# Causal attention: both halves of the turned probabilities copied by VectorE in the steps that do not end a tile

## What is computed

```python
att = jnp.einsum('bhqd,bhkd->bhqk', q, k) * hd ** (-0.5)
att = jnp.where(causal, att, -jnp.inf)
att = jax.nn.softmax(att, axis=-1)
y = jnp.einsum('bhqk,bhkd->bhqd', att, v).transpose(0, 2, 1, 3).reshape(Bb, T, C)
return y @ wo + bo
```

## Time and profile before

| | us |
|---|---|
| median of three runs | 1734.31 |
| lowest and highest run | 1730.68, 1734.47 |
| the profiled execution | 1724.97 |
| its span on the core | 1723.42 |
| TensorE matmul busy | 1594.9 |
| TensorE weight loads busy | 1322.6 |
| VectorE busy | 741.0 |
| ScalarE busy | 680.1 |
| GpSimd busy | 240.4 |
| mean granted TensorE clock over the span | 0.961 of full speed |

### The profile page before, as it was taken

One profiled execution on the slowest core, in us unless ns is written; L12 is line 12 of the kernel. 1 busy time (PEld: TensorE's weight loads), 2 busy tenths in 40 slices (PEclk: granted clock), 3 DMA queues, 4 the chain that ended last, 5 costly groups with the idle time before them and its releaser, 6 DMA issues.

```text
span 1723.4 us, 32899 instructions
## 1 busy us (share of the span) xinstructions
PE 1594.9 (93%) x12477; PEld 1322.6 (77%) x12477; DVE 741.0 (43%) x2621; ACT 680.1 (39%) x2160; POOL 240.4 (14%) x378
## 2 busy tenths in 40 slices
PE   7999989889999999999689988989999999999986
PEld 5787877689986777777488877878987777777765
DVE  2635445521025666755111137553114444344457
ACT  2614423322105757556133317543324443244432
POOL 2012200000001121211411123128000000000000
PEclk9999999989999999989699989889999999999998
DMA  9500011238601010400498920206850001000000
GB/s 324 195 1 2 1 40 37 85 108 304 139 1 52 11 44 2 176 2 2 157 321 300 318 97 23 99 31 217 300 175 1 1 1 37 1 2 1 2 1 22
DMA packets 103255, 156.41 MB, mean 91 GB/s; under 512 B 12231, under 2 KB 80959, under 8 KB 102535
## 3 DMA queue, kind: packets, MB, share of 16 engines
q1 hardware_dynamic: 97515, 143.53, 25.5%
q0 software_dynamic: 3552, 9.18, 1.6%
q10 hardware_dynamic: 2048, 1.84, 0.3%
HBM read 147.31 MB, written 11.67 MB: 92 GB/s over the span
## 4 chain that ended last, share of the span: by engine, by line
PE 66%; ACT 8%; DVE 5%; issue 3%; DMA 2%; POOL 1%; SPq 1%; DVEq 0%; ACTq 0%; POOLq 0%
PE psum L567 42%; PE psum L638 5%; ACT arena L839 5%; PE psum L622 4%; PE psum L662 4%; PE psum L916 3%; PE psum L523 3%; DMA moe_b<-in_moe_b 2%; POOL token_rows L1217 1%; PE psum L903 1%; PE psum L670 1%; DVE arena L756 1%; ACT arena L851 1%; PE psum L908 0%; SPq L985 0%
## 5 line engine op out<-in xcount | busy, mean ns | idle before, releaser
L839 ACT ACTIVATE arena<-arena,rowmin 112x375 f32<-112x375 f32 (+1 forms) x584 | 292.8, 508 | 179.3 <-DVE rowmin L756 179.1
L567 PE MATMUL psum<-arena,region 128*128 128x112 f32 (+2 forms) x1920 | 325.8, 328 | 6.5 <-DMA arena<-in_ctxT 2.5
L567 PEld LDWEIGHTS psum<-arena,region 128*128 128x128 f32 x1920 | 263.2, 197 | 69.8 <-issue 8.1
L567 PE MATMUL psum<-region,arena 128*125 128x128 f32 (+4 forms) x1632 | 234.4, 293 | 16.5 <-DVE arena L1986 4.8
L567 PEld LDWEIGHTS psum<-region,arena 128*125 128x125 f32 (+2 forms) x1632 | 197.2, 184 | 51.5 <-issue 19.3
L638 PEld LDWEIGHTS psum<-identity,arena 112*125 112x125 f32 (+1 forms) x1240 | 142.4, 177 | 63.7 <-ACT arena L851 17.2
L638 PE MATMUL psum<-identity,arena 112*125 112x112 f32 (+1 forms) x1240 | 169.2, 279 | 18.8 <-ACT arena L851 5.0
L567 PE MATMUL psum<-arena 128*128 128x128 f32 (+4 forms) x896 | 138.2, 312 | 0.8 <-DMA moe_b<-in_moe_b 0.8
L622 PE MATMUL psum<-arena 32*112 32x375 f32 (+3 forms) x912 | 133.5, 477 | 0.5 <-DVE arena L734 0.4
L567 PEld LDWEIGHTS psum<-arena 128*128 128x128 f32 (+2 forms) x896 | 124.0, 189 | 12.1 <-issue 1.6
L897 POOL COPY arena<-rinv 112x128 f32<-112x128 f32 x136 | 34.0, 293 | 595.2 <-DVE rinv L776 571.3
(11 more groups left out here) (298 smaller groups left out, 1871.3 us busy)
## 6 DMA issues: line engine op xcount, KB each, us to landing
stream<-in_moe_w SPq DMA_DIRECT2D x36, 1024.0 KB, 7.4
arena<-in_moe_w SPq DMA_DIRECT2D x36, 1024.0 KB, 7.3
arena<-in_ctxT SPq DMA_DIRECT2D x32, 375.0 KB, 4.0
stream<-in_e_wg SPq DMA_DIRECT2D x8, 512.0 KB, 4.4
stream<-in_e_wu SPq DMA_DIRECT2D x8, 512.0 KB, 5.5
stream<-in_e_wd SPq DMA_DIRECT2D x8, 512.0 KB, 6.6
region<-in_e_wg SPq DMA_DIRECT2D x8, 512.0 KB, 7.5
region<-in_e_wu SPq DMA_DIRECT2D x8, 512.0 KB, 8.2
```

The lines of the kernel that those rows point to most:

```text
L567: last = pe.matmul(dst, l, r, start=(i == 0), stop=(i == n - 1))
L839: last = act.activation(e, e, ACT.Exp, bias=rowmin[:, j, n:n + 1], scale=-1.0, accum_out=rowsum[:, j, h:h + 1])
```

## The change

In `attend_vector`, `keep_rest(r)` first copies the half of sequences 0 and 1 out of bank 4 and signals `probs_T`, and then does its own copy out of bank 5, if r is not the last step of its tile. In `attend_scalar`, `keep_probs(r)` does nothing for these steps. The last step of a tile is done as before: ScalarE copies bank 4 and VectorE bank 5.

```diff
--- before.py
+++ after.py
@@ -764,6 +764,9 @@
                 if r >= 2:
                     v.wait_ge(*p["probs_used"].at(it, r - 2))
                 if a.whole_pairs:
+                    if r % a.steps + 1 < a.steps:
+                        v.tensor_copy(a.turned(r)[0:T, 0:2, 0:2 * T], three(bank[4][0:T, 0:4 * T], 2))\
+                            .then_inc(p["probs_T"].sem, 1)
                     dst, src = a.turned(r)[0:T, 2:4, 0:2 * T], three(bank[5][0:T, 0:4 * T], 2)
                 else:
                     n = a.key_tiles - 1
@@ -841,6 +844,8 @@
                 last.then_inc(p["probs"].sem, 1)
 
             def keep_probs(r):
+                if a.whole_pairs and r % a.steps + 1 < a.steps:
+                    return
                 act.wait_ge(*p["probs_turned"].at(it, r))
                 if r >= 2:
                     act.wait_ge(*p["probs_used"].at(it, r - 2))
```

## The result

Six runs of each kernel were timed in turn: the changed kernel took 1721.13 us (median; 1719.80 to 1725.84), the kernel before 1732.74 (1730.68 to 1734.47). The ratio is 0.994, 95% interval 0.9927 to 0.9953: 0.6% faster, 10 to 12 us. The prediction had the direction and what the copies do, but less than a third of the size: 3.1 us, with 1725 as the lowest time. The profiled execution took 1721.13 us, its span 1719.6.

What follows compares the result with a forecast made beforehand. ScalarE was taken to pace the steps at 3.39 us, TensorE 0.44 behind. A -1.5, B and D -1.2 each and C +0.8 gave -3.1 us, from the median 1734.31 to 1731.2 us; range 1725 to 1737.

Steps and rivals of the forecast that it cites:

- C: Layer 1's attention over the first four sequences; first tile gains 0.82 us, second loses 1.59, together +0.8 us.
- A: Layer 0's attention over the first four sequences, with two normalisations on VectorE; forecast -1.5 us.
- B: Layer 0's attention over the second four sequences; first tile 0, second tile -1.23, together -1.2 us.
- D: Layer 1's attention over the second four sequences, with gates' arithmetic like B; forecast -1.2 us.
- B's gates: Gates' arithmetic on VectorE after step 1, 1.39 us, leaves no idle time; B's first tile gains 0.
- the case against: C's second tile: VectorE also adds tokens and paces it, so three more copies make it 1.59 us later.
- it hangs on where things fall, and I leave it out of the sum: Low clock in closings of A and C, costing 1.7 us in A; outside the sum, two stretches either way in range.
- The prediction's own sign of the clock: If the total moves over 5 us while the attentions move 3, the clock did it; closings' granted clock shows it.
- Of the rivals, the first: Clock comes back: three falls vanish (A, C and one more), gain 8.2 us, 1726.1 us; chance 0.2.
- The second: Clock falls further: C's wait grows, B's luck ends, two more slow stretches, +0.3 us, 1734.6 us; chance 0.15.
- The third: VectorE paces every tile through the pair of copies ahead of the masks: +12.7 us, 1747.0 us; chance 0.06.
- the fourth: Nothing arrives: weight transfers behind C and D set the experts' pace, 1734.3 us; chance 0.07.

Runs made afterwards that it cites:

- before_pad8: Kernel before plus eight padding products ahead of each attention's last transposes, no copy moved; ratio 0.9955, 1714.70 us against 1723.55.
- layer0_only: Kernel before with the copies moved in attentions A and B alone; ratio 0.9961 to the kernel before.
- layer1_only: Kernel before with the copies moved in attentions C and D alone; ratio 0.9994 to the kernel before.
- after_again: The changed kernel once more, unchanged; ratio 0.9957 to the kernel before, 1715.19 us.
- base_again: The kernel before once more, unchanged; ratio 1.0003 to the kernel before.
- look_before: A further profile of the unchanged kernel before, a single execution; 1733.64 us.
- change_only: The changed kernel again, unchanged, on another chip; ratio 0.994 to the kernel before (1731.34 us).
- pad_only: Same kernel as before_pad8 (eight padding products per attention, no copy moved), measured again; ratio 0.9944 to the kernel before (1731.34 us).

## Why the prediction was wrong

*The copies: right in their working, 1.4 us too small in sum.* These are starts read from the timelines, relative to the attention's first exponential. Without falls or the long C:

| | predicted | measured | from |
|---|---|---|---|
| A, first tile | -0.8 | -0.86 | second tile starts at 18.05, before 18.91 |
| A, second tile | -0.7 | -0.71 | to the last transposes 13.35, before 14.06 |
| B, first tile | 0 | -0.25 | 18.67, before 18.92 |
| B, second tile | -1.23 | -1.27 | 12.79, before 14.06 |
| C, first tile | -0.82 | -1.10 | 18.04, before 19.14 |
| C, second tile | +1.59 | +1.58 | 17.17, before_pad8 15.59 |
| D | -1.2 | -1.9 | last transposes at 31.47, before 33.33 |
| sum | -3.1 | -4.5 | |

The pair costs 2 x 0.53 us, which was the value taken; neither the dependence between the two copies nor slower reads of PSUM appeared. The Trainium skill, VectorE: DVE Perf Modes, section Specifications, puts ScalarE closer to PSUM and VectorE closer to SBUF; 0.53 against 0.41 us agrees in sign, but ScalarE was the one that paced, so the dearer engine was the right one.

A's second tile runs at 3.26 us a step as computed for VectorE with its normalisations (starts at 21.60, 24.86 and 28.12). B's gates come out as the working had them: the eight transposes were to start 9.55 us behind B's first exponential (779.87 less 770.32); they start at 9.58, 775.87 less 766.29. VectorE and TensorE's weight loads in B answer to the earlier trace rows:

```profile
773.26 0.29 DVE L2136 TENSOR_TENSOR arena<-expert_number,gate_small 112x32 f32<-112x32 f32 x2
...
774.65 0.62 DVE L768 COPY arena<-psum 112x448 f32<-112x448 f32 x1
775.18 0.61 DVE L774 COPY arena<-psum 112x448 f32<-112x448 f32 x1
```
```profile
775.87 0.76 PEld L638 LDWEIGHTS psum<-identity,arena 112*112 112x112 f32 x8 [0.61 <-DVE arena L768]
776.78 0.35 PEld L662 LDWEIGHTS psum<-arena 112*32 112x32 f32 x16
```

Of B's extra 0.25, 0.09 is there when these transposes are done (the outputs behind them start 10.49 us into B, before 10.58). The other 0.15 comes where the next transposes stand behind the key and query products: from one set of outputs to the next it was 3.41 us before (780.90 to 784.31, with a part of a wait for exponentials) and is 3.26 now (776.78 to 780.04). I had argued that nothing after the key and query products waits; something still did.

Of C's 1.10 in the first tile, 0.22 us aren't its copies': its second step starts 3.30 us after its first instead of 3.52. It does so in layer0_only too, where C has no copy moved, and doesn't in layer1_only, where it has; what C's own copies give there is 0.88. In the kernel before VectorE pauses 0.2 us between two of the masks (1044.64 to 1045.05, where two usually start 0.2 apart). Of D's 1.9, 0.36 us aren't its copies' either: in layer0_only, where D has none moved, D's second tile also starts 0.36 earlier (18.92, before 19.27). So some 0.6 of the 4.5 us came with the change but not from an attention's own copies, and why is open.

C's second tile is the case against, and it came true to 0.01 us. The exponentials of after_again start 4.45 us apart (1066.00 to 1070.45), before 3.92. Its weight loads answer to the earlier trace rows, the wait of 2.54 us is now 3.04. The profile puts it down to line 768, but TensorE waits for both copies, and the second, line 774, is the last to be ready: it starts at 1073.75, and the transposes 0.69 us later.

```profile
1068.88 0.62 DVE L768 COPY arena<-psum 112x448 f32<-112x448 f32 x1
1069.42 0.61 DVE L774 COPY arena<-psum 112x448 f32<-112x448 f32 x1
...
1073.23 0.60 DVE L768 COPY arena<-psum 112x448 f32<-112x448 f32 x1
1073.75 0.61 DVE L774 COPY arena<-psum 112x448 f32<-112x448 f32 x1
```
```profile
1071.04 0.35 PEld L662 LDWEIGHTS psum<-arena 112*32 112x32 f32 x16
1074.44 0.76 PEld L638 LDWEIGHTS psum<-identity,arena 112*112 112x112 f32 x8 [3.04 <-DVE arena L768]
```

*The step that failed: "it hangs on where things fall, and I leave it out of the sum".* The clock term was set to zero in the sum, as a matter of luck, with two stretches either way in the range. It is a term with a sign. Of the kernel before, three profiles have a fall in A's closing three times, in B's twice and in D's twice. Of the changed kernel, four profiles have none in A, B or D; C's stays. On one chip, base_again is 7.8 us longer in the four attentions than after_again (160.23 less 152.45), 4.5 by the copies and 3.3 by the falls of A and B. Against after_again, the first profile of before is 7.7 us longer in the four attentions (160.18 less 152.45): 4.5 of these are the copies; falls are the other 3.2 (A 1.7, D 1.6, C -0.1, which stays). B's fall, where it occurs, adds 1.6. The profiles with the long C differ by 9.1 us in the four attentions (look_before 170.34, change_only 161.20). Of these, 4.5 are again the copies, so the falls make 3.2 to 4.6 us, which the sum had at nothing. The medians differ by 7.1 us on the chip without the long C and by 11.6 and 10.9 on two where it occurs, so up to 2.5 us lie in stretches that the change doesn't touch. There executions of the same kernel differ by as much: the changed kernel has 38 to 44 us at 1.2 GHz before A, and A starts between 708.9 and 712.0, so I don't explain them. The prediction's own sign of the clock, a total that moves by more than 5 us while the attentions move by 3, came in kind: the total moved by 11.6, the copies by 4.5.

What TensorE did ahead of the closings goes with their clock. In the last step of A in the kernel before it waited 1.22 us for ScalarE's copy and then twice for exponentials, 2.14 us in all:

```profile
742.45 0.19 PEld L638 LDWEIGHTS psum<-identity,arena 112*112 112x112 f32 x2 [0.37 <-ACT arena L839]
743.19 0.19 PEld L638 LDWEIGHTS psum<-identity,arena 112*112 112x112 f32 x2 [0.55 <-ACT arena L839]
```

In the changed kernel the first wait is a little longer, but all of them together are 1.65 us:

```profile
740.24 0.57 PEld L638 LDWEIGHTS psum<-identity,arena 112*112 112x112 f32 x6 [1.36 <-DVE arena L768]
741.10 0.18 PEld L638 LDWEIGHTS psum<-identity,arena 112*112 112x112 f32 x2 [0.29 <-ACT arena L842]
```

So the change shortened two things: these last waits, and the 0.44 us that TensorE stood still in each step before them. Counted over all 18 profiles, by the sum of the waits in the last step:

| closings | waits in the last step, us | with a fall |
|---|---|---|
| C, not padded | 2.54 to 3.07 | 11 of 11 |
| A, B, D, copies not moved | 2.14 | 8 of 12 (A 4 of 4, B and D 2 of 4 each) |
| A, B, D, copies moved | 1.60 to 1.65 | 0 of 21 |
| all four, padded | 0 to 0.51 | 0 of 28 |

Filling the last waits was enough by itself (before_pad8, with the old steps). For the change it isn't shown whether the shorter last waits or the shorter ones in the steps before did it, since no run separates them. In C the falls came with and without the moved copies. The Trainium skill says (TensorE: Matmul & The Clock Gate, Part 1) that the low clock is the default and that activity releases it. The padded closings agree, none of which fell, with products whose results nobody reads. I had this rule and the earlier trace rows side by side and took B's 1.00 as evidence against it; it was one draw.

Of the rivals, the first came true in kind: its 8.2 us (three falls of 1.7 and the copies) is near the measured 7.1 to 11.6, with B and D in the place of C. I gave it 0.2. The second, that the clock falls further, happened in C alone (6.8 us at 1.2 GHz in after_again, and 3.4 before), also without the moved copies (layer0_only), and in after_again it cost 0.1 us only. The third is refuted by 2.98 us steps, and the fourth by the totals. The low end of the range was too high: rival 1 with the cheaper copies (-4.3) and four falls of 1.7 gives -11.1, or 1723.2, still above the measured 1721.13, and the median of before was itself 1.6 us lower in the comparison than in the runs shown.

## What to carry to other kernels

Where an engine ahead of TensorE sets the pace of short steps, its relief can pay twice, as here: once in the steps (4.5 us) and once in TensorE's clock behind them (3.2 to 4.6); cost the second term from the granted clock of several executions, and ask which waits ahead of a fall the edit shortens. Before moving work for its sake, pad the last wait: eight products per attention brought some 0.5% in this kernel with no other change, of which the attentions themselves account for 4.9 us, 0.3%. Copies go to the engine with room in that very step, even at 0.53 instead of 0.41 us, but stay where they were in a tile in which the receiving engine has other work (C).

## What was not expected of the hardware

**A standstill of 8 us in C.** In the first profile of the changed kernel, C's fourth step starts 10.0 us behind its third, instead of 3.0. VectorE's timeline has a wait that the profile puts down to "remote":

```profile
1041.80 0.61 DVE L774 COPY arena<-psum 112x448 f32<-112x448 f32 x1
1051.67 0.62 DVE L768 COPY arena<-psum 112x448 f32<-112x448 f32 x1 [7.71 <-remote]
```

The transposes that this copy reads were loaded from 1042.84 on, long before. At the same time the weight loads of TensorE's padding products, which wait for no other engine, came one or two at a time 1.4 us apart, where they usually start 0.11 apart:

```profile
1042.84 0.82 PEld L638 LDWEIGHTS psum<-identity,arena 112*112 112x112 f32 x8
...
1047.37 0.30 PEld L523 LDWEIGHTS psum<-identity 128*128 128x128 f32 x2 [1.22 <-issue]
1048.82 0.19 PEld L523 LDWEIGHTS psum<-identity 128*128 128x128 f32 x1 [1.15 <-issue]
1050.23 0.50 PEld L523 LDWEIGHTS psum<-identity 128*128 128x128 f32 x2 [1.23 <-issue]
```

GpSimd issues eight indirect gathers in this stretch, one in 1.24 us:

```profile
1045.42 0.93 POOL L1250 DMA_INDIRECT stream<-token_outputs,token_slots  x1 [0.30 <-issue]
1046.66 0.93 POOL L1250 DMA_INDIRECT stream<-token_outputs,token_slots  x1 [0.30 <-issue]
```

The kernel before has the same in look_before, where ScalarE stands still as well:

```profile
1059.38 0.62 DVE L771 COPY arena<-psum 112x448 f32<-112x448 f32 x1 [6.86 <-remote]
```
```profile
1059.37 0.53 ACT L848 COPY arena<-psum 112x448 f32<-112x448 f32 x1 [5.08 <-remote]
```

On two of the four chips of the groups above every profile has it (C is 7 to 10 us longer), on two others none has, with the same gathers at the same place, so the gathers alone aren't the cause. The kernel before took 1731 us on the former and 1722 to 1724 on the latter; the chip of the first comparison gave 1732.74 in its runs, though its one profile of before lacks the standstill and took 1724.97. So the 9.3 us by which that profile lay below the median are, it seems, this event. Why several engines stop together isn't settled; a late supply of instructions would look like this, but no run here shows it. It is in both kernels, and the ratios with it (0.994 and 0.994) and without it (0.9957) have overlapping intervals.

**The clock's falls move.** The same kernel falls in other closings from one execution to the next, and a kernel with padded closings can fall elsewhere: in pad_only 1.75 us into A, ahead of the first padded closing. A single profile prices a fall well (1.6 to 1.7 us), and its place badly.
